# The mean of a layer norm's last tile taken from TensorE by row sums of W_up, and VectorE's order of work around it

## The reference

```
h = gelu(x @ W_down[role] + b_down[role])        # x: (8, 512, 1024), W_down: (3, 1024, 512)
u = h @ W_up[role] + b_up[role]                  # W_up: (3, 512, 1024)
y = x + u
mean = y.mean(-1);  var = ((y - mean) ** 2).mean(-1)
out = (y - mean) * rsqrt(var + 1e-5) * gamma[role] + beta[role]
```

## Time and profile before

| | |
|---|---|
| median of 3 runs | 362.35 us |
| lowest and highest | 362.21 and 362.82 us |
| the profiled execution's own time | 362.48 us |
| its span (first to last instruction) | 360.7 us |
| TensorE's granted clock over the span | 0.998 |

### The profile page before, as it was taken

How to read it: one execution, slowest core, us unless ns; L and a number is a source line. 1 busy time by engine, 2 the same in 40 slices (tenths; PEclk the granted TensorE clock), 3 DMA queues, 4 the chain that set the end, 5 groups by cost and what they waited for, 6 DMA issues and landing times.

```text
span 360.7 us, 4991 instructions
## 1 busy us (share of the span) xinstructions
PE 353.2 (98%) x1559; PEld 290.2 (80%) x1559; DVE 285.6 (79%) x301; ACT 185.0 (51%) x303; POOL 59.8 (17%) x75
## 2 busy tenths in 40 slices
PE   9999999999999999999999999999999999999992
PEld 4888888888888888888888888888888888888882
DVE  3788999298993989759996699957989489893886
ACT  4785556761368415682256814476234862255133
POOL 0000222003220213102140022300232003320003
PEclk9999999999999999999999999999999999999999
DMA  6999999962999549994699927999099981745023
GB/s 187 393 408 409 410 393 358 355 237 87 333 336 362 219 121 370 330 344 172 172 363 343 353 107 244 341 360 352 40 297 348 377 315 53 240 147 204 1 115 120
DMA packets 27804, 96.61 MB, mean 268 GB/s; under 512 B 3218, under 2 KB 3858, under 8 KB 27794
## 3 DMA queue, kind: packets, MB, share of 16 engines
q1 hardware_dynamic: 23186, 81.14, 62.8%
q10 hardware_dynamic: 4608, 15.34, 11.0%
HBM read 79.70 MB, written 16.78 MB: 267 GB/s over the span
## 4 chain that ended last, share of the span: by engine, by line
PE 92%; DVE 3%; ACT 2%; issue 1%; POOL 1%; POOLq 0%; DVEq 0%; ACTq 0%
PE down_ps L311 48%; PE up_ps L318 42%; DVE rows L683 1%; PE up_ps L432 1%; DVE rows L688 1%; ACT squares L488 1%; DVE rows L742 0%; POOL rstd L603 0%; DVE up_ps L720 0%; POOLq L44 0%; ACT h_full L478 0%; ACT h_hi L480 0%; ACT neg_mean_scaled L485 0%; POOL var_eps L601 0%; DVE down_ps L705 0%
## 5 line engine op out<-in xcount | busy, mean ns | idle before, releaser
L311 PE MATMUL down_ps<-x_hi,wd_hi 128*128 128x512 f32 x256 | 81.2, 390 | 0.1
L311 PE MATMUL down_ps<-x_lo,wd_hi 128*128 128x512 f32 x256 | 80.9, 389 | 0.0
L311 PE MATMUL down_ps<-x_hi,wd_lo 128*128 128x512 f32 x256 | 80.8, 389 | 0.0
L318 PE MATMUL up_ps<-wu_hi,h_hi 128*128 128x512 f32 x248 | 76.4, 389 | 0.0
L318 PE MATMUL up_ps<-wu_lo,h_hi 128*128 128x512 f32 x248 | 76.4, 389 | 0.0
L318 PE MATMUL up_ps<-wu_hi,h_lo 128*128 128x512 f32 x248 | 76.3, 389 | 0.0
L601 POOL TENSOR_TENSOR var_eps<-var,eps 128x1 f32<-128x1 f32 x31 | 22.7, 733 | 292.0 <-ACT squares L488 292.0
L485 ACT ACTIVATE neg_mean_scaled<-row_sum 128x1 f32<-128x1 f32 x31 | 6.3, 203 | 124.7 <-DVE rows L688 124.7
L676 DVE TENSOR_TENSOR h_lo<-h_full,h_hi 128x512 fp32r<-128x512 f32 x32 | 22.2, 693 | 46.6 <-ACT h_hi L480 46.6
L311 PEld LDWEIGHTS down_ps<-x_hi,wd_hi 128*128 128x128 f32 x256 | 47.9, 188 | 11.1 <-issue 0.9
L311 PEld LDWEIGHTS down_ps<-x_hi,wd_lo 128*128 128x128 f32 x256 | 48.0, 188 | 10.0
(11 more groups left out here) (64 smaller groups left out, 274.2 us busy)
## 6 DMA issues: line engine op xcount, KB each, us to landing
wu_stage<-W_up SPq DMA_DIRECT2D x32, 512.0 KB, 7.0
rows<-x SPq DMA_DIRECT2D x32, 512.0 KB, 7.4
x_stage<-xT SPq DMA_DIRECT2D x30, 512.0 KB, 7.1
wd_stage<-W_down SPq DMA_DIRECT2D x30, 512.0 KB, 8.6
out<-rows ACTq DMA_DIRECT2D x28, 512.0 KB, 4.6
b_up_row<-b_up SPq DMA_DIRECT2D x8, 512.0 KB, 5.1
gamma_row<-gamma SPq DMA_DIRECT2D x8, 512.0 KB, 9.5
beta_row<-beta SPq DMA_DIRECT2D x8, 512.0 KB, 10.3
```

The lines of the kernel that those rows point to most:

```text
L311: return pe.matmul(down_ps[:, kc, :], wd_part[:, n, c * K + kc * P:c * K + (kc + 1) * P], x_part[:, n, c * S:(c + 1) * S], start=start, st ...
L318: mm = pe.matmul(up_ps[:, t % 2, half], h_part[:, kc, t * P:(t + 1) * P], wu_part[:, kc, half], start=(kc == 0 and h_part is h_hi and wu_p ...
```

## The change

W_up's rows are summed: ScalarE reads each of the four 128-row pieces of `wu_stage` once more with an accumulator (`sum_wu`, four passes over 1024 columns, between the variances of tiles 0 and 1 of the last sequence and ahead of them). The four sums, each with a zero beside it, are split like the weights into high part and rest (`round_wu_sum` on ScalarE, `split_wu_sum` on VectorE) and lie as columns 1024 and 1025 behind `wu_hi` and `wu_lo`, whose rows grow to 1026 numbers. TensorE's last tile now begins with columns 768 to 1025: 258 columns, of which the last but one gives the row sum of the whole up projection. ScalarE also sums the residual's row (`sum_last_residual`). The two sums together give the true mean (`last_mean`, one small VectorE instruction) when the first of the three parts is done.

With that the first mean, the recentring, the shift and POOL's square of it go. Each part of the last tile gets one pass that adds the residual and the mean, from PSUM into `h_full` (`centre_part`), ScalarE squares it from there (`part_variance`), VectorE multiplies by gamma, from `h_full` into `rows` (`scale_part`), and the finishing passes read and write `rows` (`finish_piece`). The order of the parts is now 768 to 1023, 0 to 511, 512 to 767, on TensorE and behind it.

```diff
-        wu_hi = sb("wu_hi", [P, KC, H], F32R)
-        wu_lo = sb("wu_lo", [P, KC, H], F32R)
+        wu_hi = sb("wu_hi", [P, KC, H + 2], F32R)
+        wu_lo = sb("wu_lo", [P, KC, H + 2], F32R)
+        wu_sum = sb("wu_sum", [P, KC, 2], F32)
...
+        LAST_PARTS = (POOL_PIECE,) + PIECES
+        LAST_BANKS = (down_ps[:, 0, 0:POOL_COLS], last_tile[:, PIECES[0]], last_tile[:, PIECES[1]])
+        LAST_MOVING = (slice(H - POOL_COLS, H + 2),) + PIECES
+        LAST_OUT = (down_ps[:, 0, 0:POOL_COLS + 2],) + LAST_BANKS[1:]
+        PROJECTED_SUM = down_ps[:, 0, POOL_COLS:POOL_COLS + 1]
...
                     if is_last(b) and t == NT - 1:
-                        for part, bank in zip(LAST_PARTS, LAST_BANKS):
+                        pe.wait_ge(wu_sum_split, 1)
+                        for part, bank in zip(LAST_MOVING, LAST_OUT):
...
+            def sum_wu(i):
+
+                if i == 0:
+                    act.wait_ge(var_ready, NT * (B - 1))
+                    act.wait_ge(constants_ready, 3)
+                elif i == 2:
+                    act.wait_ge(var_ready, NT * (B - 1) + 1)
+                else:
+                    act.wait_ge(wu_sum_ready, i)
+                act.activation(squares[:, :], wu_stage[:, i, :], ACT.Identity,
+                               accum_out=wu_sum[:, i, 0:1]).then_inc(wu_sum_ready, 1)
+
+            def round_wu_sum():
+                act.wait_ge(wu_sum_ready, KC)
+                act.copy(wu_hi[:, :, H:H + 2], wu_sum[:, :, :]).then_inc(wu_sum_hi_ready, 1)
+
+            def sum_last_residual():
+                act.wait_ge(biased, NT * B)
+                act.wait_ge(var_ready, NT * (B - 1) + 2)
+                act.activation(squares[:, :], rows[:, NT - 1, :], ACT.Identity,
+                               accum_out=residual_sum[:, :]).then_inc(residual_sum_ready, 1)
+
+            def part_variance(i):
+                if i == 0:
+                    act.wait_ge(var_ready, NT * B - 1)
+                act.wait_ge(last_part_centred, i + 1)
+                act.activation(squares[:, LAST_PARTS[i]], centred[:, (NT - 1) % 2, LAST_PARTS[i]], ACT.Square,
+                               scale=H ** -0.5, accum_out=part_var[:, i:i + 1]).then_inc(part_var_ready, 1)
 
             def scale_last_columns():
                 t = NT - 1
-                act.wait_ge(scaled, NT * B + 2)
+                act.wait_ge(last_part_scaled, 1)
                 act.wait_ge(rstd_ready, NT * B)
-                act.mul(centred[:, t % 2, POOL_PIECE], LAST_BANKS[2], rstd[:, t:t + 1]).then_inc(act_scaled, 1)
+                act.mul(centred[:, t % 2, POOL_PIECE], rows[:, t, POOL_PIECE], rstd[:, t:t + 1]).then_inc(act_scaled, 1)
...
+                if last:
+                    sum_wu(0)
+                    sum_wu(1)
                 variance(b, 0)
+                if last:
+                    sum_wu(2)
+                    sum_wu(3)
+                    round_wu_sum()
                 variance(b, 1)
+                if last:
+                    sum_last_residual()
...
+            def split_wu_sum():
+                dve.wait_ge(wu_sum_hi_ready, 1)
+                dve.tensor_tensor(wu_lo[:, :, H:H + 2], wu_sum[:, :, :], wu_hi[:, :, H:H + 2].bitcast(F32),
+                                  ALU.subtract).then_inc(wu_sum_split, 1)
...
+            def last_mean():
+
                 dve.wait_ge(last_part_ready, 1)
+                dve.wait_ge(residual_sum_ready, 1)
+                dve.tensor_scalar(last_neg_mean[:, :], PROJECTED_SUM, residual_sum[:, :], -1.0 / H,
+                                  ALU.add, ALU.mult).then_inc(last_mean_ready, 1)
+
+            def centre_part(i):
+                dve.wait_ge(last_mean_ready, 1)
+                dve.wait_ge(last_part_ready, i + 1)
+                dve.scalar_tensor_tensor(out=centred[:, (NT - 1) % 2, LAST_PARTS[i]], in0=LAST_BANKS[i],
+                                         scalar=last_neg_mean[:, :], in1=rows[:, NT - 1, LAST_PARTS[i]],
+                                         op0=ALU.add, op1=ALU.add).then_inc(last_part_centred, 1)
+
+            def scale_part(i):
+                dve.wait_ge(last_part_centred, i + 1)
+                dve.tensor_tensor(rows[:, NT - 1, LAST_PARTS[i]], centred[:, (NT - 1) % 2, LAST_PARTS[i]],
+                                  gamma_row[:, LAST_PARTS[i]], ALU.mult).then_inc(last_part_scaled, 1)
+
+            def finish_piece(i):
                 t = NT - 1
                 dve.wait_ge(rstd_ready, NT * B)
+                dve.wait_ge(last_part_scaled, i + 2)
+                dve.scalar_tensor_tensor(out=rows[:, t, PIECES[i]], in0=rows[:, t, PIECES[i]],
+                                         scalar=rstd[:, t:t + 1], in1=beta_row[:, PIECES[i]],
+                                         op0=ALU.mult, op1=ALU.add).then_inc(normed, 1)
...
                 for t in range(NT - 2):
                     sum_tile(b, t)
                     centre_tile(b, t)
+                    if t == 1:
+                        split_wu_sum()
                     finish_tile(b, t)
                 sum_tile(b, NT - 2)
+                last_mean()
+                centre_part(0)
                 centre_tile(b, NT - 2)
-                sum_first_half()
+                scale_part(0)
                 finish_tile(b, NT - 2)
-                sum_part(1)
-                sum_part(2)
-                last_norm()
+                centre_part(1)
+                centre_part(2)
+                scale_part(1)
+                scale_part(2)
+                finish_piece(0)
+                finish_piece(1)
```

More of the change, by code:

```diff
@@ L78, in bass_role_adapter_layernorm @@
         neg_mean_scaled = sb("neg_mean_scaled", [P, NT], F32)
-        part_sums = sb("part_sums", [P, 3], F32)
-        first_mean = sb("first_mean", [P, 2], F32)
-        neg_shift = sb("neg_shift", [P, 1], F32)
+        residual_sum = sb("residual_sum", [P, 1], F32)
+        last_neg_mean = sb("last_neg_mean", [P, 1], F32)
         first_var_eps = sb("first_var_eps", [P, 1], F32)
         two_var_eps = sb("two_var_eps", [P, 1], F32)
-        square_shift = sb("square_shift", [P, 1], F32)
-        known_var = sb("known_var", [P, 1], F32)
         squares = sb("squares", [P, H], BF16)
@@ L139, in bass_role_adapter_layernorm @@
         summed = sem("summed")
[L140 to L143, removed]
+        wu_sum_ready = sem("wu_sum_ready")
+        wu_sum_hi_ready = sem("wu_sum_hi_ready")
+        wu_sum_split = sem("wu_sum_split")
+        residual_sum_ready = sem("residual_sum_ready")
+        last_mean_ready = sem("last_mean_ready")
+        last_part_centred = sem("last_part_centred")
+        last_part_scaled = sem("last_part_scaled")
         act_scaled = sem("act_scaled")
         pool_normed = sem("pool_normed")
-        square_shift_ready = sem("square_shift_ready")
-        known_var_ready = sem("known_var_ready")
         scaled_mean_ready = sem("scaled_mean_ready")
@@ L489, in variance @@
                                scale=H ** -0.5, accum_out=var[:, t:t + 1]).then_inc(var_ready, 1)
[L491 to L507, removed]
@@ L592, in _ @@
             steps(B - 1)
-            last_variance()
+            part_variance(0)
+            part_variance(1)
+            part_variance(2)
             scale_last_columns()
@@ L612, in last_inverse_deviation @@
                 pool.tensor_tensor(two_var_eps[:, :], part_var[:, 1:2], first_var_eps[:, :], ALU.add).then_inc(two_var_eps_ready, 1)
-                pool.wait_ge(shift_ready, 1)
-                pool.tensor_tensor(square_shift[:, :], neg_shift[:, :], neg_shift[:, :], ALU.mult).then_inc(square_shift_ready, 1)
-                pool.wait_ge(square_shift_ready, 1)
+            def last_inverse_deviation():
+                t = NT - 1
                 pool.wait_ge(two_var_eps_ready, 1)
-                pool.tensor_tensor(known_var[:, :], two_var_eps[:, :], square_shift[:, :],
-                                   ALU.subtract).then_inc(known_var_ready, 1)
-                pool.wait_ge(known_var_ready, 1)
                 pool.wait_ge(part_var_ready, 3)
-                pool.tensor_tensor(var_eps[:, t:t + 1], part_var[:, 2:3], known_var[:, :], ALU.add).then_inc(var_eps_ready, 1)
+                pool.tensor_tensor(var_eps[:, t:t + 1], part_var[:, 2:3], two_var_eps[:, :], ALU.add).then_inc(var_eps_ready, 1)
                 pool.wait_ge(var_eps_ready, NT * B)
@@ L640, in _ @@
                 inverse_deviation(B - 1, t)
+            add_first_variance()
+            add_second_variance()
             last_inverse_deviation()
@@ L690, in sum_tile @@
                                          accum_out=row_sum[:, t:t + 1]).then_inc(summed, 1)
-            def sum_first_half():
-                t, half = NT - 1, slice(0, BANK)
-                dve.wait_ge(biased, NT * B)
+            def last_mean():
                 dve.wait_ge(last_part_ready, 1)
-                dve.scalar_tensor_tensor(out=last_tile[:, half], in0=last_tile[:, half], scalar=1.0,
```

(18 more changed lines are left out.)

14 lines of the change are left out of this document (6 added, 8 removed).

## The result

The changed kernel takes 368.25 us (median of 5 runs, 368.09 to 368.51) against 362.35 before: a ratio of 1.0159, 95% interval 1.0144 to 1.0174. The forecast was 363.2 with a range up to 363.6: it is slower, as forecast, but by 5.9 us and not by 0.8.

The account below looks back on a forecast made before the run. TensorE, busy 98% of a 360.7 us span, was taken as the bound up to the tail. Tail terms 0.33 + 0.25 + 0.25 = 0.83 us on 362.35 gave 363.2 us, range 362.5 to 363.6.

Parts of the forecast that it names:

- the price of the weights' rows: Up projection, all 32 tiles: 1026-number rows shift operands off round addresses; taken as 0, bad case +3.7 us; rival, 4%.
- The third tile's finishing held up by POOL: Tail: POOL's var_eps and rstd wait under VectorE passes, so finish_tile starts at 352.85 in place of 352.52: +0.33 us.
- From there to F: Tail, finish_tile's start to F: a 512-column pass and its square now follow finish_tile; 4.22 against 3.97 us, +0.25.
- F: Instant in the tail when rstd is there and the finishing passes start: 356.49 before, forecast 357.07, 0.58 us later.
- POOL's last addition: After F: held by VectorE's second finishing piece, it ends at F + 1.71 in place of F + 1.46: +0.25 us.
- the prediction's first part: Tail: the chain ending last runs through POOL's addition, 1.46 us after F; the change is worth its effect on both.
- The two rivals on POOL: Tail: last addition not held, +0.53, 362.9 us, 28%; POOL nowhere held, +0.2, 362.55 us, 8%.
- ScalarE's and VectorE's added passes: Weights' sums, rounding, split and residual's sum fit into idle time around tile variances; split has 1.4 us to spare.

Follow-up runs that it names:

- run with VectorE's order changed back: The run with PSUM, with VectorE centring the third tile ahead of the last tile's first part and that part's gamma after the third tile's finishing: 362.98 us.
- the other three: The kernel with the round pitch (363.01 us), the run with VectorE's order changed back (362.98 us), and the latter with four 256-column last-tile parts, two centred before finish_tile (362.60 us).
- the kernel with the round pitch: The changed kernel with a weights' row pitch of 1088 numbers and wu_sum allocated behind the other small tensors: 363.01 us, ratio 1.0016.
- the run with PSUM: The kernel with the round pitch, with scale_part writing into PSUM and finish_piece reading it from there: 363.13 us, ratio 1.0027.
- the four runs with the round pitch: The run with PSUM and the other three, all with a weights' row pitch of 1088 numbers: 362.60 to 363.13 us.

## Why the prediction was wrong

**The step that failed** is the price of the weights' rows. The prediction listed it as a rival ("No row shows such a read ... so I take 0 and hold 5 ns for a bad case: +3.7 us"), gave it 4%, and left its upper bound out of the range. Measured are 5 to 7 ns on each matmul of the up projection, and 5.26 us are lost before the tail. The range was said to take in "the upper bounds"; this one, of +3.7 us, it left out, and even that was too small. The reason given for 0, that only contiguous runs are read, was no evidence: the reads that became slow are contiguous too. Even the rival's mechanism was only half right. It spoke of the weights' own starts; what counts is where the streamed operand lies against the stationary one. The change upsets that in two ways, by the pitch and by pushing h_hi and h_lo 96 bytes on, and in the kernel before the second alone costs 5.5 us.

The Trainium skill, page "SBUF — State Buffer", section "Who interferes with whom", gives TensorE two read ports of SBUF, one for the moving operand and one for the weights' loading, and calls them independent. The runs here don't bear the last out: moving one operand by 32 bytes against the other costs 5.3 us, moving both by 96 costs 0.6. Measurement decides. What inside the chip makes the two reads meet, no run here shows.

**The tail, term by term.** The forecast of 0.83 was 0.33 + 0.25 + 0.25.
- The third tile's finishing held up by POOL: 358.00 - 353.60 = 4.40 after the last tile, 4.18 before: +0.22 where 0.33 was forecast. The mechanism is right, as the run with VectorE's order changed back shows (4.20). The term was too large, since `last_mean` and the first centring started up to 0.1 earlier than worked out.
- From there to F: 362.25 - 358.00 = 4.25 against 3.97, +0.28 where 0.25 was forecast. That hit is in part luck. The squares were done in 0.12 less than the sum had it: from the first one's start to the end of the last reading 1.13 (359.98 to 361.11), forecast 1.25. But POOL's `two_var_eps` was held (0.47 in place of 0.19), and `var_eps` needs it: it started only at 361.40, 0.29 after that reading, where 0.07 was forecast. The sum had no term for this.
- POOL's last addition: 0.27 later after F, 0.25 forecast. Right in the trace and shown by the run that removes it, but **it doesn't set the end**, and there the prediction's first part was wrong ("The chain that ends last runs through POOL's addition"). The span ends 360.7 - 356.49 = 4.2 us after F before, 366.4 - 362.25 = 4.15 after, 361.6 - 357.37 = 4.2 in the run where the addition ends 0.33 earlier, and 4.15 to 4.22 in the other three. The DMA engines show why. Here are, for the kernel with the round pitch and then for the run with PSUM, SP's two last stores, POOL's being the second, and the microsecond from F + 2.0 to F + 3.0; the last two numbers are the mean busy share of the core's 16 DMA engines and GB/s (the 0.50 ahead of them is TensorE's granted clock; it has no work left):

```profile
357.40 1.31 SPq L294 DMA_DIRECT2D out<-rows  x2
358.62:359.62 1.00, 0.00 (x0) 0.00 (x0) 0.00 (x0) 0.00 (x0) 0.00 (x0) 0.50 1.02 350
```

```profile
358.15 0.98 SPq L294 DMA_DIRECT2D out<-rows  x2
359.37:360.37 1.00, 0.00 (x0) 0.00 (x0) 0.00 (x0) 0.00 (x0) 0.00 (x0) 0.50 1.03 351
```

The three stores carry 512 KB together, the first of them released by VectorE's first finishing piece. In the kernel before, the changed kernel and the four runs with the round pitch the engines are busy all through that microsecond (shares of 1.01 to 1.03), move their last packet at F + 3.2, and the last landing is at F + 3.7. POOL's store is issued 1.76 after F in the first of the two and lands 1.9 later, and 1.43 after F in the second and lands 2.3 later: whichever it is, the engines are through with the three stores at the same time. So the term of 0.25 was right for the addition and worth nothing for the time.

So of the tail's 0.83 us the 0.5 us at F remain, which the kernel with the round pitch shows as a whole: +0.45 us. The two rivals on POOL were decided as forecast (it is held), and ScalarE's and VectorE's added passes were hidden as forecast: tile 0's variance still waits 4.21 us, and the weights' sums are rounded by 348.98, 4.6 us ahead of TensorE's last tile. Of the 5.9 us, about 5.1 lie in TensorE's longer phases, 0.2 in the first phase, and about 0.5 in the tail; with the operands placed as before, 5.2 us of it went.

## What to carry to other kernels

Treat the byte offset between a matmul's streamed and stationary operand as part of the schedule: when a buffer grows or a small tensor is slipped in between large ones, pad it so that both operands keep their places modulo 256 bytes (differences of 256 bytes and a row pitch of 17 times 256 were free here), and put small tensors behind the large ones. The sign is a matmul group whose mean duration has grown by a few ns with no idle time in front; multiplied by its count it can outweigh any gain in a tail. A cost that no row shows gets both bounds in the range, above all when it is multiplied by hundreds. And where the last stores keep the DMA engines busy, an earlier issue of one of them need not end the span earlier: here 0.33 us gave nothing.

## What the runs showed of the hardware that was not expected

- A 512-column matmul with a 128-column weight load beside it takes 389 ns by the profile, and 394 to 397 ns when the starts of its two operands differ by 32, 64, 96 or 128 bytes; at a difference of 0 or 256 bytes it is 389 to 390. Over an up phase of 96 matmuls that is 21.76 against up to 22.5 us. It holds for both projections of this kernel.
- The last 512 KB, in three stores, end on the 16 DMA engines 3.2 us after F in six kernels, whether the last store is issued 1.43 or 1.76 us after F.
- This one was forecast, and a run now shows it: a POOL instruction over 256 columns, started under a VectorE piece with two inputs in SBUF, took 1.02 us in place of 0.72; with that piece reading PSUM it took 0.72. VectorE's own pieces kept their length (1.15 and 1.14 us for the two).
